# Weight slots moved against the activations in SBUF, and the softmax kept in one tile

## The reference, cut to what matters

```python
q = einsum('bsd,de->bse', h, wq)            # 128 of each head's 192 columns are used
k, v = ...                                  # the same with wkv
scores = einsum('bqhd,bkhd->bhqk', q, k) * 192 ** -0.5
scores = where(causal, scores, -1e30)
probs = softmax(scores)                     # 32 x 32 of each batch and head
x = x + einsum('bse,ed->bsd', attn(probs, v), wo)
```

## The kernel before, in words

| tile | before | after |
|---|---|---|
| `yc` (y) | 384 | 384 |
| `wh`, slot 0 and 1 | 384 | 384 |
| `wh`, slots 2, 3, 4 | 384 | 448 (y + 64) |
| `wh`, slots 5, 6, 7 | 384 | 64 (y + 192) |
| `wo`, `o_hi`, `o_lo`, `qk`, `probT`, `v_tok` | 384 | 384 |
| `kept`, v's combination j | 128 + 32 j | 128 + 32 j |

## Time and profile before

### The profile page before, as it was taken

One profiled execution on the slowest core, in us unless ns is written; L12 is line 12 of the kernel. 1 busy time (PEld: TensorE's weight loads), 2 busy tenths in 40 slices (PEclk: granted clock), 3 DMA queues, 4 the chain that ended last, 5 costly groups with the idle time before them and its releaser, 6 DMA issues. The chain is left out here.

```text
span 2122.5 us, 36889 instructions
## 1 busy us (share of the span) xinstructions
PE 2094.0 (99%) x11922; PEld 1813.4 (85%) x11922; DVE 1386.1 (65%) x2619; ACT 718.6 (34%) x1444; POOL 1255.3 (59%) x1315
## 2 busy tenths in 40 slices
PE   7999999999999999999999999999999999999999
PEld 5888888988888898989888898989887778878887
DVE  8767777676777767665656566566666766655444
ACT  5333232332323232332323233232323644443332
POOL 4578575767767676776758576776746642114120
PEclk9999999999999999999999999999999999999999
DMA  7421212211121226111111211111112200001110
GB/s 242 155 62 46 55 53 75 54 52 47 49 52 44 78 60 219 55 41 41 40 40 44 64 49 40 40 40 40 40 62 79 89 21 0 0 1 40 40 40 20
DMA packets 122615, 122.28 MB, mean 58 GB/s; under 512 B 35249, under 2 KB 101457, under 8 KB 120497
## 3 DMA queue, kind: packets, MB, share of 16 engines
q1 hardware_dynamic: 91697, 109.87, 16.7%
q10 hardware_dynamic: 29568, 7.34, 1.7%
q0 software_dynamic: 1280, 4.20, 0.7%
HBM read 108.13 MB, written 13.28 MB: 57 GB/s over the span
## 5 line engine op out<-in xcount | busy, mean ns | idle before, releaser
L215 PE MATMUL psum<-yc,wh 128*128 128x512 f32 x904 | 360.5, 399 | 0.3 <-PEq L264 0.3
L217 PE MATMUL psum<-yc,wh 128*128 128x512 f32 x904 | 352.4, 390 | 0.0
L216 PE MATMUL psum<-yc,wh 128*128 128x512 f32 x904 | 352.4, 390 | 0.0
L1464 DVE TENSOR_TENSOR resid<-psum,resid 128x512 f32<-128x512 f32 x248 | 171.2, 691 | 137.4 <-PE psum L217 133.0
L215 PE MATMUL psum<-kept,yc 128*128 128x256 f32 x896 | 254.7, 284 | 2.4 <-DVE u L1414 1.6
L1017 POOL TENSOR_TENSOR wh<-wh_f,wh 128x256 fp32r<-128x256 f32 x256 | 189.7, 751 | 105.6 <-ACT wh L983 103.6
L216 PE MATMUL psum<-kept,yc 128*128 128x256 f32 x896 | 251.5, 281 | 0.0
L217 PE MATMUL psum<-kept,yc 128*128 128x256 f32 x896 | 251.3, 280 | 0.0
L1017 POOL TENSOR_TENSOR wh<-raw,wh 128x256 fp32r<-128x256 f32 x192 | 142.5, 742 | 98.7 <-ACT wh L983 98.7
L217 PEld LDWEIGHTS psum<-yc,wh 128*128 128x128 f32 x904 | 169.7, 188 | 35.9
L215 PEld LDWEIGHTS psum<-yc,wh 128*128 128x128 f32 x904 | 170.1, 188 | 31.7 <-issue 0.7
(11 more groups left out here) (367 smaller groups left out, 4926.5 us busy)
## 6 DMA issues: line engine op xcount, KB each, us to landing
raw<-in_attn_w SPq DMA_DIRECT2D x96, 512.0 KB, 4.9
wo_f<-in_attn_w SPq DMA_DIRECT2D x31, 512.0 KB, 4.0
hankel<-kernel_rows SPq DMA_DIRECT2D x32, 256.0 KB, 4.7
y_parts<-stage ACTq DMA_DIRECT2D x56, 128.0 KB, 2.3
yc<-y_parts SPq DMA_DIRECT2D x7, 1024.0 KB, 5.1
resid<-in_xT SPq DMA_DIRECT2D x4, 1024.0 KB, 9.6
outT<-wide SPq DMA_DIRECT2D x16, 256.0 KB, 2.6
kept_f<-in_l_w SPq DMA_DIRECT2D x3, 1024.0 KB, 5.8
```

What stands on the lines that cost most here:

```text
L215: pe.matmul(out, w[0], x[0], start=start, stop=False)
L216: pe.matmul(out, w[0], x[1], start=False, stop=False)
L217: return pe.matmul(out, w[1], x[0], start=False, stop=stop)
L1464: dve.tensor_tensor(part, psum[:, 5 + (GH + m) % 3, :], part, ALU.add).then_inc(tail_free, 1)
```

## The change

`wh` becomes a flat tile of 8 slots x 512 floats and 128 floats more. `part` adds 0, 16 or 48 floats (0, 64 or 192 bytes) to the slot's place. The tile `ex` (1 KB in each partition) goes: `exps`, `soft_divide`, `soft_turn` and their halves at the end work in `sc`. `soft_shift` and `end_shift`, which overwrite `sc`, wait in addition for the `prob_ready` of the softmax before. `last_wo` takes the same first 2048 floats of `wh` as before. Each engine has the same instructions in the same order in both programs; the tiles behind `wh` lie 512 bytes further on up to `sc`, and those behind `ex` 512 bytes nearer.

```diff
@@ class HeadWeights
-        self.wh_raw, self.wh = overlaid(stack, "wh", [P, 8, 2, 2 * DH])
+        self.wh_raw, self.wh = overlaid(stack, "wh", [P, 8 * 4 * DH + 128])
@@ def part
         slot = j + (1 if j == 6 and kind in ("H1", "H3") else 0)
-        return (self.wh_raw if plain else self.wh)[:, slot, low, :]
+        at = slot * 4 * DH + (0, 0, 16, 16, 16, 48, 48, 48)[slot] + low * 2 * DH
+        return (self.wh_raw if plain else self.wh)[:, at:at + 2 * DH]
@@ def attention
-        ex = sb(ctx, "ex", [P, NBK, SEQ])
-        last_wo_raw, last_wo = (w[:].rearrange("p j l n -> p (j l n)")[:, 0:2 * GH * DIM].rearrange("p (l n) -> p l n", l=2)
+        last_wo_raw, last_wo = (w[:, 0:2 * GH * DIM].rearrange("p (l n) -> p l n", l=2)
@@ def exps
-                act.activation(ex[:], sc[:], ACT.Exp).then_inc(exp_done, 1)
+                act.activation(sc[:], sc[:], ACT.Exp).then_inc(exp_done, 1)
@@ def soft_shift
                 dve.wait_ge(scores_done, sm + 1)
+                dve.wait_ge(prob_ready, sm)
@@ def soft_divide
-                then(dve.tensor_reduce(total, ex[:], AX_X, ALU.add))
+                then(dve.tensor_reduce(total, sc[:], AX_X, ALU.add))
                 then(dve.reciprocal(inv, total))
-                then(dve.tensor_tensor(ex[:], ex[:], inv.unsqueeze(2).broadcast_to([P, NBK, SEQ]), ALU.mult))
+                then(dve.tensor_tensor(sc[:], sc[:], inv.unsqueeze(2).broadcast_to([P, NBK, SEQ]), ALU.mult))
@@ def soft_turn
-                    ins = dve.transpose(probT[q, slot, :, b * SEQ:(b + 1) * SEQ], ex[q, :, :])
+                    ins = dve.transpose(probT[q, slot, :, b * SEQ:(b + 1) * SEQ], sc[q, :, :])
...
```

More of the change, by code:

```diff
@@ L1278, in end_exps @@
                 act.wait_ge(shifted, END + i + 1)
-                act.activation(ex[:, half(i), :], sc[:, half(i), :], ACT.Exp).then_inc(exp_done, 1)
+                act.activation(sc[:, half(i), :], sc[:, half(i), :], ACT.Exp).then_inc(exp_done, 1)
             def end_high(i):
@@ L1608, in end_shift @@
                 dve.wait_ge(scores_done, END + i + 1)
+                dve.wait_ge(prob_ready, END)
                 blocks = psum[:, 3 + i, :].rearrange("p (s n) -> p s n", n=P)
@@ L1625, in end_divide @@
                 dve.wait_ge(exp_done, END + i + 1)
-                then(dve.tensor_reduce(total, ex[:, half(i), :], AX_X, ALU.add))
+                then(dve.tensor_reduce(total, sc[:, half(i), :], AX_X, ALU.add))
                 then(dve.reciprocal(inv, total))
-                then(dve.tensor_tensor(ex[:, half(i), :], ex[:, half(i), :], inv.unsqueeze(2).broadcast_to([P, SUBS, SEQ]),
+                then(dve.tensor_tensor(sc[:, half(i), :], sc[:, half(i), :], inv.unsqueeze(2).broadcast_to([P, SUBS, SEQ]),
                                        ALU.mult))
@@ L1634, in end_turn @@
                     q = slice(b * SEQ, (b + 1) * SEQ)
-                    ins = dve.transpose(probT[q, 1, half(i), b * SEQ:(b + 1) * SEQ], ex[q, half(i), :])
+                    ins = dve.transpose(probT[q, 1, half(i), b * SEQ:(b + 1) * SEQ], sc[q, half(i), :])
                 ins.then_inc(prob_ready, 1)
```

## The result

The changed kernel takes 2135.53 us (median of 4 runs, 2134.4 to 2140.34), the kernel before beside it 2126.62 (4 runs, 2125.03 to 2127.56). The ratio is 1.0045, with a 95% interval of 1.0033 to 1.0058: slower by 8.9 us, where 11.9 were forecast.

What follows compares the result with a forecast made beforehand. TensorE's own matmul sequence was taken as the bound, so only pitch counts: 12.7 us for 1920 moved weight loads less 0.8 already lost gives +11.9 us, 2138.7 us against the median of 2126.83; range 2114 to 2144.

Steps and rivals of the forecast that it cites:

- The bound and the reading by pitch: TensorE's own matmul sequence sets the end; only the pitch matters, TensorE's waits stay and VectorE's waits for it grow.
- The price of 64: H products with weights 64 bytes from y: +6.6 ns per matmul, read from layer one's rows with 512 columns.
- The price of 192: H products with weights 192 bytes from y: the same +6.6 ns per matmul; slots 2 to 7 together +12.7 us.
- What is lost already: Slots 2 and 3 behind score groups: first two matmuls already slow, 5 ns less to lose each, -0.8 us.
- The return to 0: Slots 0, 1 and output pieces behind products at other distances: put at nothing, at most 2.6 us kept for the range.
- Two readings of the rows: TensorE waits only 1.5 us once inside the passes; layer one's good-pitch rows stand between slow ones, against other engines' influence.
- V's law holds for H: Rival 1, slots 2 to 7: 64 and 192 are faster places, -5.2 to -14.0 us; 32%.
- the place is without effect: Rival 2: weight loads under H matmuls cost the same anywhere, 2126.8 us; 13% with cases where 64 and 192 cancel.
- the Trainium skill's rule of the independent read ports: TensorE reads moving operand and weights through two independent ports, so the weights' place would be without effect.
- slots 0 and 1 lose their lock for good: Rival 3: slots 0 and 1 and output pieces lose the good pitch too, +17.0 us, 2143.8; 5%.
- The softmax: One-tile softmax: 65 added waits ahead of the shift are hidden and in-place exponentials have the same sizes, 0.

Runs made afterwards that it cites:

- the map: Small program of matmul chains alone, 30 at each distance, other engines idle: 512 columns 226.6 ns at 0, 233.1 at 64, 229.4 at 192.
- The chain of states: Small program, chains of 36 matmuls at one place behind 18 of another kind: 512 columns at 0 return to 226.7 ns after 6 matmuls behind 512 at 64.

## Why the prediction was right, and which terms were off

The forecast was +11.9 us and the medians give +8.9, inside the range and in the direction that was put at 55%. The mechanism was the one forecast, a longer pitch of the moved weights' matmuls; several of its terms were off.

*The bound and the reading by pitch* were right. TensorE's count and clock stayed, its waits changed by no more than they do from run to run, VectorE waits more for TensorE, and the difference of the spans is found again in the pitches.

*The price of 64* (+6.6 ns, from layer one) was right: slot 4 shows 233.3 - 226.9 = 6.4 ns, and with all six slots at 64 the kernel is 14.4 us slower. The rows of another stage could serve because the map repeats after 256 bytes: the distances 320 and 64 of the earlier trace rows are both the place of 64. The prediction, which counted modulo 512, took them for near rows only.

*The price of 192* was the failed term: "any other costs 6.6 ns more" was a rule drawn from distances of 32 and 64 and applied to one that no row had. 192 costs 229.1 - 226.7 = 2.4 ns in slots 5 to 7 and 229.4 - 226.6 = 2.8 ns in the map. In place of 768 x 6.6 = 5.1 us the slots' sums show 2.6, and 1.8 without the wait in the first pass.

*What is lost already* was taken as 0.8 us over slots 2 and 3. Their pitches rise by 4.1 and 5.4 ns where slot 4's rise by 6.4: about 384 x 2.3 + 384 x 1.0 = 1.3 us, somewhat more than the term. The 1152 matmuls at 64 were put at 7.6 - 0.8 = 6.8 us and give 6.0.

*The return to 0* was put at nothing, with up to 2.6 us kept for the range. It costs 0.7 us in slots 0 and 1 and 1.2 us in the output pieces. The chain of states shows its size for 512 columns: six matmuls, which is the length of a whole product. The sentence that V products are followed by such pieces was true and no reason: the pieces behind V products have 229.8 ns before and after. What lost are the pieces behind slots 2, 3 and 4, which had 226.7 to 228.5 ns and now have some 231; they make up the 1.2 us.

So the misses partly cancel, which is luck: 11.9 - 2.5 (192) - 0.8 (64) + 1.9 (the return) = 10.5 us. With the table's +0.9 for everything else, -0.4 for V products and fp32 and -0.9 for the earlier start it is the spans' 10.1. The medians' 8.9 lie 1.2 us under that; the interval of the ratio reaches from 7.0 to 12.3 us.

*Two readings of the rows* were not exact. Inside the passes TensorE waits somewhat more than the 1.5 us named: seven V pitches over 260 ns, 5.9 us in all, hold waits too. And the earlier trace rows stand ahead of the earlier trace rows, not between them; the map, with no other engine at work, settles what they were called upon for.

*The rivals.* That V's law holds for H (faster) falls: with 512 columns no distance is under 226.6 ns. But its premise, that 256 columns prefer another place, is what the map shows (113.6 at 64). That the place is without effect falls twice, by the small program, in which no other engine works, and by the same edit at 64, 192 and 240, which gives 1.0066, 1.0025 and 0.9997. So the Trainium skill's rule of the independent read ports (SBUF — State Buffer, "Who interferes with whom") does not hold as a statement on time for this form of matmul: weights loaded under a matmul cost 0 to 8 ns by their place. Where it speaks of other engines the runs don't contradict it: alone on the chip 512 columns take 226.6 ns at 0 and 233.1 at 64, in the kernel 226.9 and 233.3. That slots 0 and 1 lose their lock for good falls as well: their median pitch is still 227 and 228 ns.

*The softmax* at nothing was right, for the reason given. VectorE's timeline after, from a turn to the next shift:

```profile
1064.59 1.78 DVE L1453 STREAM_TRANSPOSE probT<-sc 32x256 f32<-32x256 f32 x4
...
1067.24 0.69 DVE L1414 TENSOR_TENSOR v_tok<-psum,kept_f 128x512 f32<-128x512 f32 x1 [0.86 <-PE psum L217]
1067.85 1.71 DVE L1432 SCALAR_TENSOR_TENSOR sc<-psum,consts 32x256 f32<-32x256 f32 x4
```

The shift starts 3.26 us behind the turn's start, as in the earlier trace rows (1058.18 to 1061.44): the turn that it now waits for is long over. ScalarE's exponentials keep their length:

```profile
L1270 ACT ACTIVATE sc<-sc 128x256 f32<-128x256 f32 x63 | 26.4, 419 | 139.5 <-DVE sc L1438 139.5
```

## What to carry to other kernels

Where TensorE is busy to the end and loads new weights for every matmul, the pitch itself is worth reading from the starts, and the place of the loaded weights against the moving operand, modulo 256 bytes, is part of the layout: measure it with a small program for the form and length at hand before shifting tiles. A rule drawn from two distances is no rule for a third, and what such a chain gives holds in the kernel only if what runs just ahead of it is the same.

## What the runs showed of the hardware

- In the map, fp32r matmuls of 512 columns with a load each have a pitch of 226.7 ns at 0, 240 and 256, of 229.4 at 192 and 229.9 at 176, and of 232 to 234 at the others, with a period of 256 bytes; 16 has 227 or 233 by what ran ahead. 256 columns have other favourites (113.6 at 64), and 128 columns take 111.7 ns at any place.
- The pitch depends on what ran ahead. The same 36 matmuls ran at 226.7 or 233.3 ns, and others at 113.3 or 117.8, for as long as the chain lasted; in the kernel before, the same V product ran at 118.0 or 113.3.
- Behind fp32 matmuls the first pitch of 512 columns was 313 to 319 ns, and at distance 0 the good one came back after seven matmuls.

Why the memory behaves so is open. Two streams that are read in turn and fall into or out of step would fit a period in bytes and a memory of what ran ahead, but no run here looks inside; that weights of half the width lose as much at their worst place speaks against a loss that simply counts the bytes loaded.
